# A decoder layer on one core: new task order and maxima's bank in cross-attention; eight-head score units and a one-pass product with B in the feed-forward

## The reference, cut to what matters

```
# cross-attention, 16 heads of 16 channels, quantised projections of queries and outputs
q = w8a8(x, wq, bq);  k = cond @ wk.T + bk;  v = cond @ wv.T + bv
attn = softmax(q @ k.T * 0.25 + mask);  x = layernorm(x + w8a8(attn @ v, wo, bo))
# feed-forward
attn = attention(rmsnorm(x, ln1), Wq, Wk, Wv, Wo)        # causal, 16 heads of 16
mod  = 0.1 * tanh(attn @ A)                              # A: 256 x 16
h    = rmsnorm(x, ln2)
gate = silu(h @ W_in.T + mod * (h @ A) @ B)              # B: 16 x 1024
out  = layernorm(2 * x + (gate * (h @ W_up.T)) @ W_down.T)   # the stage and the layer both add x
```

## Time and profile before

| | us |
|---|---|
| time, median of 3 runs (lowest, highest) | 4096.11 (4090.36, 4101.38) |
| the profiled execution | 4115.7 |
| its span | 4114.0 |
| PE busy over the span | 3691.4 (90%) |
| DVE, ACT, POOL busy | 2596.5 (63%), 1596.1 (39%), 648.8 (16%) |

### The profile page before, as it was taken

How to read it: one execution, slowest core, us unless ns; L and a number is a source line. 1 busy time by engine, 2 the same in 40 slices (tenths; PEclk the granted TensorE clock), 3 DMA queues, 4 the chain that set the end, 5 groups by cost and what they waited for, 6 DMA issues and landing times. The chain is left out here.

```text
span 4114.0 us, 95372 instructions
## 1 busy us (share of the span) xinstructions
PE 3691.4 (90%) x34364; PEld 2671.0 (65%) x34364; DVE 2596.5 (63%) x6225; ACT 1596.1 (39%) x2842; POOL 648.8 (16%) x784
## 2 busy tenths in 40 slices
PE   7999999994899989989898998899899859999998
PEld 6988999993556655655655555565565636666665
DVE  4444444444677767767777777677777756666665
ACT  3222223221344544444444444444445433332322
POOL 0000000003011111101111011111111103332222
PEclk9999999997899999999999999899999979999999
DMA  2000000003546454654646555364554520000000
GB/s 94 13 13 12 9 7 8 12 9 76 95 90 106 90 103 84 109 94 82 108 80 111 91 97 101 73 113 89 95 102 93 93 60 5 13 12 17 15 12 13
DMA packets 121819, 256.97 MB, mean 62 GB/s; under 512 B 18564, under 2 KB 99276, under 8 KB 118364
## 3 DMA queue, kind: packets, MB, share of 16 engines
q1 hardware_dynamic: 113136, 243.95, 31.5%
q10 hardware_dynamic: 8300, 7.69, 0.7%
HBM read 99.79 MB, written 9.83 MB: 27 GB/s over the span
## 5 line engine op out<-in xcount | busy, mean ns | idle before, releaser
L1391 DVE CUSTOM_DVE_ANT_0 ca_rowmax<-ca_rowmax,ca_msk 100x1024 f32<-100x1024 f32 (+1 forms) x1024 | 929.2, 921 | 383.6 <-PE ca_rowmax L1159 377.1
L1097 ACT ACTIVATE ca_prob<-ca_unit 128x800 f32<-128x800 f32 x640 | 534.6, 835 | 558.7 <-PE ca_unit L1283 558.6
L1159 PE MATMUL ca_rowmax<-ca_ks,ca_qs 96*100 96x512 bf16 (+1 forms) x1536 | 518.6, 408 | 81.0 <-DMA ca_ks<-ca_ks 47.6
L1283 PEld LDWEIGHTS ca_unit<-ca_qs,ca_ks 99*128 99x128 bf16 (+1 forms) x6144 | 356.0, 100 | 212.2 <-issue 124.8
L1002 POOL TENSOR_TENSOR ca_key_part<-ca_key_rest,ca_key_part 128x512 bf16<-128x512 f32 (+1 forms) x192 | 211.5, 1102 | 1680.3 <-ACT ca_key_part L1064 1680.3
L1246 PE MATMUL ca_acc<-ca_prob,ca_vaug 128*17 128x100 f32 x12288 | 444.6, 258 | 21.1 <-issue 20.8
L1283 PE MATMUL ca_unit<-ca_qs,ca_ks 99*128 99x100 bf16 (+1 forms) x6144 | 439.4, 212 | 24.1 <-issue 15.3
L1141 PE MATMUL ca_ring<-ca_wvT,ca_ctxT 128*128 128x256 f32 (+1 forms) x1536 | 418.2, 419 | 0.9 <-ACT ca_qs L1075 0.6
L1141 PEld LDWEIGHTS ca_ring<-ca_wvT,ca_ctxT 128*128 128x128 f32 (+1 forms) x1536 | 314.9, 207 | 79.7 <-issue 17.8
L1132 PE MATMUL ca_ring<-ca_ctxT,ca_wkT 128*128 128x512 f32 (+1 forms) x768 | 346.1, 573 | 2.3 <-ACT ca_ctxT L1048 2.3
L1159 PEld LDWEIGHTS ca_rowmax<-ca_ks,ca_qs 96*100 96x100 bf16 x1536 | 154.7, 128 | 243.8 <-issue 173.1
(11 more groups left out here) (260 smaller groups left out, 6598.3 us busy)
## 6 DMA issues: line engine op xcount, KB each, us to landing
ca_ks<-ca_key_part SPq DMA_DIRECT2D x768, 90.2 KB, 4.1
ca_ks<-ca_ks SPq DMA_DIRECT2D x64, 722.0 KB, 5.7
ca_ctx<-in_ctx SPq DMA_DIRECT2D x32, 1408.0 KB
ca_ks<-ca_ks SPq DMA_DIRECT2D x64, 361.0 KB, 8.9
ca_msk<-in_mask_BxSxS_ff SPq DMA_DIRECT2D x32, 564.1 KB
sa_w_stage<-in_L_attn_w_qkv SPq DMA_DIRECT2D x12, 512.0 KB, 5.4
sa_x_in<-in_x ACTq DMA_DIRECT2D x8, 400.0 KB
sa_x_res<-in_x SPq DMA_DIRECT2D x8, 400.0 KB
```

Of the source, the lines that this page charges most:

```text
L1097: act.activation(prob[:, s, :], unit[:, :, 0:QUAD * N], ACT.Exp).then_inc(bc.freed[0], 1)
L1159: last = pe.matmul(rowmax[0:N, s0:s1], qs[0:STACK, par, h, :], ks[0:STACK, par, h, s0:s1], start=True, stop=True)
L1283: return pe.matmul(unit[0:rows(t0 + k), k, j * N:(j + 1) * N], ks[:, par, h, keys(k)], qs[:, par, h, :], start=(j == 0), stop=True, skip_g ...
L1391: dve.tensor_tensor_reduce(rowmax[0:N, s0:s1], rowmax[0:N, s0:s1], msk[:, par, s0:s1], 1.0, -3.0e38, ALU.add, ALU.max, top[:, bank, h:h + ...
```

## The change

Cross-attention: the tasks of `slots` get another order; `mr` goes from the score bank `bc` to the `ml` bank of `bm`; the values' copy goes from VectorE to ScalarE without its bias, which VectorE adds once per batch to the output (`eo`); the last pair's exponential is one instruction; the context's load moves behind the placing of the second half. Feed-forward: units of eight heads (8 per group), whose scores are four products of 32 rows in four banks, with two masked copies of the keys instead of eight; two buffers instead of three; elementwise instructions over 800 columns; `up` and the transposes share two banks; A and B are loaded three times at rows (columns) 0, 32, 64, so that the product with B is one one-pass product of high, low and high parts.

```
     slots = {
         0: [("mh", 6), ("ct", 0, 0), ("ct", 0, 1), ("ml", 6)],
-        1: [("eo",), ("kp", 0, 0)],
-        2: [("mh", 7), ("kp", 0, 1), ("km", 0, 0)],
-        3: [("ml", 7), ("ct", 1, 0), ("ct", 1, 1), ("ex",), ("km", 0, 1)],
-        4: [("mh", 8), ("kp", 1, 0), ("ml", 8), ("ey",)],
-        5: [("mr", 1), ("mh", 9), ("kp", 1, 1), ("km", 1, 0)],
-        6: [("ml", 9), ("ct", 2, 0), ("ct", 2, 1), ("km", 1, 1), ("ez",)],
-        7: [("mh", 10), ("kp", 2, 0), ("ml", 10)],
-        8: [("mh", 11), ("kp", 2, 1), ("km", 2, 0)],
-        9: [("ml", 11), ("vp", 0), ("km", 2, 1)],
-        10: [("mh", 12), ("qq",), ("ml", 12)],
-        11: [("mr", 2), ("qx",), ("mh", 13), ("vp", 1), ("qp",)],
-        12: [("ml", 13)],
-        13: [("mh", 14), ("vp", 2), ("ml", 14), ("qs", 0)],
-        14: [("mh", 15), ("qs", 1), ("ma",)],
-        15: [("ml", 15), ("vp", 3)],
-        16: [("mh", 0), ("ml", 0)],
-        17: [("mr", 3), ("mh", 1), ("vp", 4), ("mf",)],
-        18: [("ml", 1)],
-        19: [("mh", 2), ("ml", 2)],
-        20: [("mh", 3), ("vp", 5)],
-        21: [("ml", 3)],
-        22: [("mh", 4), ("ml", 4)],
-        23: [("mr", 0), ("mh", 5)],
-        24: [("ml", 5)],
+        1: [("eo",), ("kp", 0, 0), ("mh", 7)],
+        2: [("ml", 7), ("kp", 0, 1), ("km", 0, 0), ("ct", 1, 0), ("ct", 1, 1)],
+        3: [("ex",), ("mh", 8), ("kp", 1, 0), ("km", 0, 1)],
+        4: [("ml", 8), ("ey",), ("kp", 1, 1), ("km", 1, 0), ("ct", 2, 0), ("ct", 2, 1)],
+        5: [("mr", 1), ("mh", 9), ("kp", 2, 0), ("km", 1, 1)],
+        6: [("ml", 9), ("kp", 2, 1), ("km", 2, 0), ("mh", 10), ("ez",)],
+        7: [("ml", 10), ("vp", 0), ("km", 2, 1)],
+        8: [("mh", 11), ("ml", 11), ("qq",)],
+        9: [("vp", 1), ("mh", 12)],
+        10: [("ml", 12), ("qx",), ("mh", 13)],
+        11: [("mr", 2), ("vp", 2), ("qp",), ("ml", 13)],
+        12: [("mh", 14), ("ml", 14)],
+        13: [("vp", 3), ("mh", 15)],
+        14: [("ml", 15), ("qs", 0), ("qs", 1), ("ma",)],
+        15: [("vp", 4)],
+        16: [("mr", 3), ("mh", 0), ("ml", 0)],
+        17: [("mh", 1), ("mf",)],
+        18: [("ml", 1), ("mh", 2)],
+        19: [("ml", 2), ("mh", 3)],
+        20: [("ml", 3), ("vp", 5)],
+        21: [("mh", 4), ("ml", 4)],
+        22: [("mr", 0), ("mh", 5)],
+        23: [("ml", 5)],
+        24: [],
     }
...
-        bm = Banks(nc, sems, "ca_top", top_order, lambda t: int(t[0] == "ml"),
+        bm = Banks(nc, sems, "ca_top", top_order, lambda t: int(t[0] in ("ml", "mr")),
...
+                elif task[0] == "vp":
+                    bank = bn.bank(task)
+                    bn.wait_full(act, task, b)
+                    ...
+                        v_out(TL, 0, 2).then_inc(bn.freed[bank], 1)
...
                 put(1, (1, 2))
+                if more:
+
+                    bn.wait_full(sp, ("ct", 2, C - 1), b)
+                    sp.sem_inc(sp_passed, 1)
+                    load_ctx(b + 1)
                 repeat(1)
...
+                    chain.link(dve.tensor_tensor(o, o, bias_row[0:N, 1, :], ALU.add))
                     quantise(dve, chain, o, o_st[:, 0:1], o_st[:, 1:2], o_st[:, 2:3], x_sc[:], x_int[:])\
...
+    place = {t: n % RING for n, t in enumerate(before)} | {t: 4 + n % 2 for n, t in enumerate(during)}
+    place |= {t: (n + 4) % RING for n, t in enumerate(after)}
+    place |= {("s", u): SCORES for u in range(UNITS)} | {("o", b): RING + b % 2 for b in range(G)}
...
+                            bk.wait_all_out(pe, low_before, g)
...
+                        for r in range(PAIRS):
+                            quadrant = slice(32 * r, 32 * r + 32)
+                            out_v = scored[0:N, r, :].rearrange("p (h n) -> p h n", h=2)[:, :, 0:N]
+                            last = pe.matmul(out_v, qT[quadrant, c, b * N:(b + 1) * N],
+                                             kz[quadrant, c, :, b * N:(b + 1) * N], start=True, stop=True)
...
-                        pe.matmul(ps[bank][:, 0:T], b_w[:, f * P:(f + 1) * P], wT[:], start=False, stop=True)\
+                        pe.matmul(ps[bank][:, 0:T], b_s[:, f * P:(f + 1) * P], w_s[:], start=False, stop=True)\
...
+                bk.wait_out(act, ("ua",), g)
+                act.activation(w_s[:], wT[:], ACT.Copy).then_inc(w_high, 1)
...
+                dve.wait_ge(w_high, g + 1)
+                dve.tensor_tensor(w_s[64:64 + R, :], wT[64:64 + R, :], w_s[64:64 + R, :].bitcast(F32), ALU.subtract)\
+                    .then_inc(w_done, 1)
```

More of the change, by code:

```diff
@@ L1065, in do_task, with v_out @@
                         .then_inc(mid_out, 1)
+                elif task[0] == "vp":
+                    bank = bn.bank(task)
+                    bn.wait_full(act, task, b)
+                    t = 2 * task[1]
+                    def v_out(r, n0, n1):
+                        return act.activation(
+                            vaug[0:r, par, t + n0:t + n1, :, 0:DH],
+                            ring[bank][0:r, n0 * D:n1 * D].rearrange("p (t h d) -> p t h d", t=n1 - n0, h=H), ACT.Copy)
+                    if rows(t + 1) == TL:
+                        v_out(TL, 0, 2).then_inc(bn.freed[bank], 1)
+                    else:
+                        v_out(TL, 0, 1)
+                        v_out(last_rows, 1, 2).then_inc(bn.freed[bank], 1)
                 elif task[0] == "qx":
@@ L1079, in do_task @@
                     h0 = task[1] * QUAD
-                    bank = bc.bank(task)
-                    bc.wait_full(act, task, b)
+                    bm.wait_full(act, task, b)
                     act.activation(qs[STACK:FULL, par, h0:h0 + QUAD, :].rearrange("p h n -> p (h n)"),
-                                   unit[STACK:FULL, 0, :].bitcast(BF16)[:, 0:QUAD * N], ACT.Copy)\
-                        .then_inc(bc.freed[bank], 1)
+                                   rowmax[STACK:FULL, 2 * 512:3 * 512].bitcast(BF16)[:, 0:QUAD * N], ACT.Copy)\
+                        .then_inc(bm.freed[bm.bank(task)], 1)
                 elif task[0] == "ex":
@@ L1093, in do_round @@
                     return
-                t, s = 2 * (p % PER_QUAD), slice(2 * (p % 2), 2 * (p % 2) + 2)
                 bc.wait_full(act, ("u", p), b)
[L1096 to L1101, removed]
+                act.activation(prob[:, 2 * (p % 2):2 * (p % 2) + 2, :], unit[:, :, 0:QUAD * N], ACT.Exp)\
+                    .then_inc(bc.freed[0], 1)
             run_turns(act, do_task, do_round)
@@ L1717, in group @@
                     evacuate(act, qT[:, c, :], ("q", c), g)
-                for step in range(UNITS + 4):
+                for step in range(UNITS + 3):
                     u = step - 1
@@ new lines, in group @@
+                        last.then_inc(bk.filled[SCORES], 1)
+                        if u == 0:
+                            pe.wait_ge(w_lows, len(halves))
+                            for cc in range(C):
+                                bk.wait_out(pe, ("ht", cc), g)
+                        project(g, ("up", u), up_s, hT, u)
+                    u = step - 2
+                    if 0 <= u < UNITS:
+                        pe.wait_ge(prob_done, UNITS * g + u + 1)
+                        for half in range(2):
+                            tile = ("pt", u, half)
+                            bank = bk.bank(tile)
+                            bk.wait_empty(pe, tile, g)
+                            for j in range(QUAD):
+                                last = pe.transpose(ps[bank][0:N, j * N:(j + 1) * N], prob[:, u % 2, half * QUAD + j, :],
+                                                    ident[0:N, 0:N])
+                            last.then_inc(bk.filled[bank], 1)
@@ L1831, in group @@
                                 bk.wait_out(pe, ("v", n), g)
[L1832 removed]
+                        if c == 0:
                             bk.wait_empty(pe, ("o", b), g)
[L1834 to L1838 removed]
+                        for half in range(2):
+                            bk.wait_out(pe, ("pt", u, half), g)
+                            quad = 2 * c + half
+                            for j in range(QUAD):
+                                last = pe.matmul(ps[bank][32 * j:32 * j + DH, quad * N:(quad + 1) * N],
+                                                 v[:, b, quad * QUAD + j, :], probT[:, u % 2, half, j * N:(j + 1) * N],
+                                                 start=True, stop=True)
                         last.then_inc(pv_done, 1)
```

278 lines of the change are left out of this document (125 added, 153 removed).

## The result

The changed kernel takes 4167.2 us (4159.1 to 4168.3, 4 runs) against 4098.7 us (4090.4 to 4104.6, 4 runs) beside it: ratio 1.016, 95% interval 1.014 to 1.019. The forecast was 4070 us, faster. The time is inside the range (3945 to 4170) and is the one that rival B gave (4162). The profiled execution has a span of 4166.5 us against 4114.0.

What follows compares the result with a forecast made beforehand. TensorE was taken to set the pace, with its waits and lowered clock counting. Cross-attention +26 us and feed-forward -52 us gave -26, from 4096 to 4070 us, range 3945 to 4170.

Steps and rivals of the forecast that it cites:

- rival B: Cross-attention: the stop at `ct 1,1` in round 2 lowers the clock in nearly every batch; 4162 us, chance 0.25.
- the clock's term: Cross-attention: of 3.6 us lost per batch to low clock, 2.8 goes and 1.8 comes back, -1.0.
- sign of being wrong: Cross-attention: the prediction is wrong if the batch changes by more than 3 us either way.
- Waits at the full clock: Cross-attention: new TensorE waits of 7.8 us against 6.0 us removed, net +1.8 us per batch.
- What goes: Cross-attention: waits for `mr`, lone `ml` rounds, the keys' DMA and the query disappear, 6.0 us per batch.
- the walk: Cross-attention: step-through of the new task order and SP queue; 25.7 us between key tasks against 23.4 for the DMAs.
- Product with B: Feed-forward gate steps: one one-pass product replaces two fp32 passes, saving 6.1 us per group; step 1.25 us.
- Scores: Feed-forward attention: four 32-row score products take 0.45 us per unit; bounds 0.4 side by side, 1.4 one after another.
- rival C: Feed-forward: the scores' row groups do not run side by side, unit 4.1 to 4.2 us; 4094 us, chance 0.13.
- GpSimd: Feed-forward attention: its instruction over 800 columns takes between 1.4 and 1.6 us.
- Attention part: Feed-forward: units gain 2.9 us, later first unit and drain lose 2.4, net 0.5 gained per group; ends -2.5 and +2.5.
- Rival A: Cross-attention: the waits simply go, as VectorE has slack in the new order; 3884 us, chance 0.17.

Runs made afterwards that it cites:

- e3_ct_later: Changed kernel with six cross-attention tasks re-ordered, among them `kp 0,1` ahead of `ml 7` and the `ct` 1 and 2 transposes one round later: 3949.2 us, ratio 0.967.
- e6_mr_bank: Kernel before with only `mr` moved to the bank of the lows (`mr 3` one place up): 4109.0 us, ratio 1.002.
- e11_load: Kernel before with only the next batch's context load moved between the two halves of the key stack's transfers: 4107.4 us, ratio 1.0005.
- e1_ff_only: Changed kernel with the cross-attention of before, so only the feed-forward is changed: 4053.8 us, ratio 0.990.
- e4_filled_wait: Changed kernel with 44 unread matmuls of 112 columns ahead of each of `ct 1,1` and `ct 2,1`: 4072.7 us, ratio 0.997.

## Why the prediction was wrong

The failing step is the clock's term: "With the DMA wait some 2.8 of it goes; the waits of 2.2+0.8 us within 4 us bring a fall of their own, and the 1.8 at `mh 13` sometimes one: 1.8 come back. -1.0." The first half holds: without stops, 1.93 us of low clock are left (`e3_ct_later`), a loss of 1.0 us. What came back was 10.63-1.93 = 8.7 us of low clock, a loss of 4.3 us, not 1.8. I gave the fall in round 2 a place and half a price, and the second stop, in round 4, none. In the trace the clock's loss went from 4.0 (7.94 x 1/2; I had 3.6, from the rounded mean clock) to 5.3 us a batch: +1.3 where -1.0 stood. That is 2.3 x 32 = 74 us, and the sum would have been 4144 us; the waits' +0.3 a batch and the feed-forward's 5 us make most of the rest. By the prediction's own sign of being wrong, a batch that changes by more than 3 us, cross-attention failed it with 3.56. Rival B had this mechanism, this place and 5.5 us; it deserved the larger chance, since the earlier trace rows already showed a fall of that size behind a wait of 2.06 us.

- Waits at the full clock: +1.8 forecast, +2.1 measured. `ct 1,1` and `ct 2,1` 4.1 forecast, 4.3 found. `mh 8` 0.8, found 0.5. `mh 13` and the reductions of rounds 16 to 22 3.4, found 1.4 at L1168 and 1.15 at `mr 0`, which I had not named.
- What goes: the DMA wait, `mr`'s wait for ScalarE and the query's all went. But the 2.6 for `mr` was too much even for the wait itself (the earlier trace rows have 2.1), and no gain of the bank as such: alone the move is worth nothing (`e6_mr_bank`). The load's new place alone doesn't take the DMA wait away (`e11_load`), which fits the walk, where the order did it.
- Product with B: 6.1 us a group forecast, 12.92-6.90 = 6.02 found; step 1.25 forecast, 3630.12-3628.86 = 1.26 found.
- Scores: 0.45 taken, 0.60 as one instruction group and 3475.05-3474.52 = 0.53 from start to start in `e1_ff_only`: the row groups run side by side, and rival C is out. The speed-up of 3.07 for four row groups that the Trainium skill states (TensorE: Matmul & The Clock Gate, Part 3) had made an estimate of 0.43 us. The drain at a change of tiling mode, which the Trainium skill states without a figure (TensorEngine Tiling (Array Packing), Key Properties), had made an estimate near 0.6. The trace's 0.53 lies between the two.
- GpSimd 1.4 to 1.6 us forecast, 1.52 found; unit 3.7 forecast, 3.74 and 3.43 found.
- Attention part: -0.5 us a group forecast, +1.8 found, within the bound of 2.5 but for another cause: the clock fell behind the fill's and the tail's waits (2.58 and 2.13 us), to 10.9 us of low time in the part. With the tail filled and the first unit earlier the part is 1.0 us under the kernel before.
- Rival A was half right on another kernel: the order can be had without the stops, at 3949 us.

## What to carry to other kernels

Price an idle stop of TensorE at its length plus the low clock behind it (half of that stretch at most): here two stops of 4.3 us together cost 6.8 us a batch, the first 5.3 for its 2.8. Before moving a product ahead of its bank's reader, look what stands ahead of that reader on its own engine: exchanging `kp 0,1` with `ml 7` and moving one pair of transposes was worth 171 us. Where a wait can't be taken away, work that nothing reads can hold the clock, if it writes to a bank that nobody uses. And after a task is moved to spare a wait, look in the trace whether the wait is gone or stands at the bank's next user: `mr 0`'s 1.16 us became 0.53 and 0.80.

## What the runs showed that I had not expected

- Filling the waits of 2.8 and 1.5 us without shortening them made the kernel 94 us faster (44 matmuls of 112 columns, twice a batch).
- Moving `mr 0` one round later to spare a wait of 1.16 us a batch put two shorter ones, 1.33 us together, in its place and made the kernel 25 us slower: the low clock is 4.2 us a batch with it and 1.8 without.
- Behind a stop of 1.5 us there were 21 low stretches in 30 batches with the other stop 12 us ahead of it, and 10 with that stop away.
- In `e4_filled_wait` the dummies start in columns 400 to 511 of the accumulators' bank while the sums in columns 0 to 399 are open, and those sums come out otherwise. Whether the start flag does it was not tried apart; the dummies of the later kernels go into a bank without open sums.
- Some 1.8 us of low clock a batch remain. In `e3_ct_later` nine low stretches begin in the 30 batches: six 2.3 to 2.6 us behind the end of the 1.16 us wait at `mr 0`, one behind the 0.86 us at `mh 13`, and two at a batch's end, around an idle time of over 4 us for which the profile names nobody. Why the same wait brings the clock down in some batches and not in others stays open, and no run filled it.
